# One loop over all laps, a wider class of packets from an earlier step, x loaded into the output's place and copied by ScalarE, b2 added by a product on TensorE

## The reference

```python
agg = segment_sum(edge_attr, dst, num_segments=6250)      # (200000, 128) -> (6250, 128)
h = concatenate([x, agg, u[batch]], axis=1)                # batch is all zeros: u[0] everywhere
h = relu(h @ W1 + b1)
y = x + (h @ W2 + b2)
return (y - mean(y)) / sqrt(var(y) + 1e-5)                 # over the 128 features
```

## Time and profile before

| | |
|---|---|
| median of 3 runs | 275.88 us (275.78 to 275.94) |
| the profiled execution: its own time | 276.12 us |
| its span, first to last instruction | 274.4 us |
| granted TensorE clock over the span | 0.938 |
| busy: TensorE, its weight loads | 213.2 us (78%), 168.7 us (61%) |
| busy: VectorE, ScalarE, GpSimd | 177.2 us (65%), 50.8 us (19%), 41.5 us (15%) |
| DMA | 110.06 MB, mean 401 GB/s |
| HBM read, written | 106.63 MB, 3.20 MB |

### The profile page before, as it was taken

One profiled execution on the slowest core, in us unless ns is written; L12 is line 12 of the kernel. 1 busy time (PEld: TensorE's weight loads), 2 busy tenths in 40 slices (PEclk: granted clock), 3 DMA queues, 4 the chain that ended last, 5 costly groups with the idle time before them and its releaser, 6 DMA issues.

```text
span 274.4 us, 15313 instructions
## 1 busy us (share of the span) xinstructions
PE 213.2 (78%) x6767; PEld 168.7 (61%) x6767; DVE 177.2 (65%) x435; ACT 50.8 (19%) x100; POOL 41.5 (15%) x49
## 2 busy tenths in 40 slices
PE   0874899987886449999884789895898897867872
PEld 0763687855655347877653658674766676655751
DVE  7842285793674997596874436959928769465542
ACT  0410122311211201122210211322022212121210
POOL 6400020030210012040300200300303003030020
PEclk9998699999999859999999599999599999999997
DMA  7999999999999999999999999999999999999994
GB/s 252 391 396 401 400 401 404 402 401 405 402 406 402 401 402 402 404 401 415 416 418 409 416 412 414 421 415 416 418 426 428 422 425 432 418 430 422 429 393 174
DMA packets 28863, 110.06 MB, mean 401 GB/s; under 512 B 2008, under 2 KB 3374, under 8 KB 26926
## 3 DMA queue, kind: packets, MB, share of 16 engines
q1 hardware_dynamic: 25588, 105.83, 95.9%
q10 hardware_dynamic: 3258, 4.00, 4.0%
HBM read 106.63 MB, written 3.20 MB: 400 GB/s over the span
## 4 chain that ended last, share of the span: by engine, by line
PE 58%; issue 13%; DVE 12%; DMA 12%; POOL 1%; ACT 1%; DVEq 1%; POOLq 0%; ACTq 0%
PE rows_ps L860 31%; PE cols_ps L872 14%; DMA slots<-in_edge_attr 12%; PE hid_ps L904 4%; PE hid_ps L886 3%; DVE tall_ids L687 3%; PE hid_ps L895 3%; PE hid_ps L880 2%; ACT rows L444 1%; DVE hot L615 1%; DVE z L678 1%; DVE first_of_pair L570 1%; POOL rstd L408 1%; DVE dst_local L583 1%; DVE high L696 1%
## 5 line engine op out<-in xcount | busy, mean ns | idle before, releaser
L860 PE MATMUL rows_ps<-slots,hot 64*32 64x128 f32 x6240 | 113.4, 285 | 35.7 <-issue 23.4
L860 PEld LDWEIGHTS rows_ps<-slots,hot 64*32 64x32 f32 x6240 | 93.6, 110 | 53.5 <-issue 50.7
L641 DVE TENSOR_TENSOR agg_t<-agg_t,cols_ps 128x128 f32 (+1 forms) x65 | 21.5, 331 | 84.1 <-PE cols_ps L872 83.8
L872 PE MATMUL cols_ps<-row_hot,rows 128*128 128x128 f32 (+1 forms) x260 | 56.3, 341 | 11.4 <-ACT rows L444 6.3
L615 DVE TENSOR_TENSOR hot<-edge_node,iota 128x768 f32<-128x768 f32 x65 | 61.8, 952 | 2.5 <-issue 1.6
L444 ACT ACTIVATE rows<-rows_ps 128x256 f32<-128x256 f32 x65 | 25.0, 384 | 177.3 <-PE rows_ps L860 170.1
L872 PEld LDWEIGHTS cols_ps<-row_hot,rows 128*128 128x128 f32 x260 | 40.8, 198 | 25.3 <-ACT rows L444 13.1
L408 POOL TENSOR_TENSOR rstd<-var_eps,minus_half 128x4 f32<-128x4 f32 (+1 forms) x13 | 16.6, 1275 | 196.7 <-DVE var_eps L672 196.7
L631 DVE TENSOR_TENSOR row_hot<-row_node,iota 128x256 f32<-128x256 f32 (+1 forms) x65 | 38.4, 591 | 0.0
L399 POOL TENSOR_TENSOR z<-x_rows,b_all 128x512 f32<-128x512 f32 (+1 forms) x13 | 17.2, 1323 | 29.8 <-PE hid_ps L880 29.8
L678 DVE TENSOR_SCALAR z<-z,moments,rstd (+1 forms) x49 | 17.2, 410 | 1.1 <-POOL rstd L408 1.0
(11 more groups left out here) (119 smaller groups left out, 70.3 us busy)
## 6 DMA issues: line engine op xcount, KB each, us to landing
slots<-in_edge_attr SPq DMA_DIRECT2D x65, 1536.0 KB, 14.9
x_rows<-in_x ACTq DMA_DIRECT2D x11, 256.0 KB
out<-z SPq DMA_DIRECT2D x11, 256.0 KB
dst_int<-in_dst SPq DMA_DIRECT2D x1, 384.0 KB, 3.9
dst_int<-in_dst ACTq DMA_DIRECT2D x1, 384.0 KB, 4.6
x_rows<-in_x ACTq DMA_DIRECT2D x1, 192.0 KB
out<-z SPq DMA_DIRECT2D x1, 192.0 KB
rest_slot<-in_edge_attr ACTq DMA_DIRECT2D x1, 128.0 KB, 8.5
```

Of the source, the lines that this page charges most:

```text
L641: V.tensor_tensor(cols, cols, cols_ps[:, 0:n], ALU.add).then_inc(added, 1)
L860: done = T.matmul(rows_ps[i][c * SPAN:(c + 1) * SPAN, h, 0:feats], hot[j][part, c * RUN + r, :], slots[part, j, c, r * feats:(r + 1) * fea ...
L872: done = T.matmul(cols_ps[:, 0:n], rows[i][:, h, :], row_hot[j][:, h, 0:n], start=(h == 0), stop=(h == HALVES - 1))
```

## The change

- `DENSE` goes from 30 to 25 and `TALL` from 50 to 48, so steps 25 to 29 come in pieces of 6144 instead of 3072 bytes, and steps 48 and 49 in pieces of 12288 instead of 6144.
- TensorE and VectorE each have one loop for all laps (`one_lap`). Every step but the last has 224 columns. `level2` stands behind the next `level1` throughout, but `level2` of a lap's fourth step stands ahead of the fifth `level1`, because the last three steps of a lap now share two sets of buffers (`SETS`).
- `rows_ps` has two sets instead of three. In the room, the turned x (`turn_bank`) and the second product (`y_bank`) get banks of their own.
- x is loaded into `z`, two laps ahead, and ScalarE copies it to `x_rows` (`stage_x`) for turning. GpSimd's `bias_add` is gone. `product2` begins with a product of a row of ones and b2 repeated four times, 512 columns wide, in the same sum.
- Blocks begin at row 128: block 0 now has the last 490 rows, in three pieces, and block 11 is a plain one.
- The extra product on iota in the last lap (L953 before) is gone, as are the waits of TensorE for `plan_made`.
- The ids of the `TALL` steps are turned one quarter at a time, in laps 3 to 6, and brought home in lap 7.
- VectorE and SyncE load `plan` and branch before the end: VectorE in the last lap behind the `add` of step 59, SyncE ahead of the last store.

```diff
-SETS = (0, 1, 0, 1, 2)
-DENSE_LAP = 6
-DENSE = DENSE_LAP * LAP
-TALL = 10 * LAP
+SETS = (0, 1, 0, 1, 1)
+DENSE = 5 * LAP
+TALL = 48
...
@@ sync
-            store(final)
-
             with sp.If(plan_now < 1):
+                store(final)
...
+            with sp.If(plan_now > 0):
+                store(final)
@@ gpsimd
+            G.memset(z[:, 0, :, :], 0.0).then_inc(x_zero, 1)
...
-            def bias_add(seq, i):
...
@@ scalar
             def load_x(seq):
+                if seq == 0:
+                    act.wait_ge(x_zero, 1)
                 i = seq % places
-                if seq:
-                    act.wait_ge(z_ready, seq)
...
+                for memory, home in pieces_of(i, x, lambda parts, r0, r1: z[parts, i, r0:r1, :].rearrange("p r f -> p (r f)")):
+                    act.dma_start(home, memory).then_inc(x_in[i % 2], 16)
+
+            def stage_x(seq):
+                i = seq % places
+                m = rows_of(i)
+                act.wait_ge(x_in[i % 2], x_landed(seq // places, i))
+                A.activation(x_rows[:, 0:m, :], z[:, i, 0:m, :], ACT.Copy).then_inc(x_staged, 1)
...
             for lap in range(laps):
                 for j in range(LAP):
                     t = lap * LAP + j
+                    if t:
                         copy_rows(t)
+                    if j == 1:
+                        if lap:
+                            relu(lap - 1)
+                        copy_x(lap)
+                    elif j == 3 and lap + 1 < final:
+                        load_x(lap + 2)
                     elif j == 4 and lap < final:
+                        stage_x(lap + 1)
@@ vector
+            with dve.Fori(1, laps - 1) as lap:
+                one_lap(lap, counts(lap), range(-1, LAP - 1))
+            last_at = step_bases((laps - 1) * LAP - 1, LAP)
+            one_lap(laps - 1, last_at, range(-1, 0))
+            def ending():
+                one_lap(laps - 1, last_at, range(0, LAP - 1))
+                add(held, 0, DENSE_COLS)
+                residual(final, final)
+                variance(final, final)
+                normalise(final, final)
...
+            plan_now = general_if(dve)
+            with dve.If(plan_now < 1):
+                ending()
                 general()
+            with dve.If(plan_now > 0):
+                ending()
@@ tensor
             def product2(seq, i):
...
+                T.matmul(y_bank[:, 0:n], ones[0:1, :], b2_rows[:, :, :].rearrange("a r f -> a (r f)")[:, 0:n], start=True, stop=False)
                 pe.wait_ge(hid_made, seq + 1)
                 for r in range(rows_of(i)):
-                    done = T.matmul(y_ps[:, r, :], hid[:, r * P:(r + 1) * P], w2_sb[:, :], start=True, stop=True)
+                    done = T.matmul(y_ps[:, r, :], hid[:, r * P:(r + 1) * P], w2_sb[:, :], start=False, stop=(r == rows_of(i) - 1))
...
+            def one_lap(lap):
                 counts(lap)
                 for j in range(LAP):
                     t = lap * LAP + j
                     if j == 4:
+                        level2(t - 1, j - 1, COLS)
                     level1(t, lap, j)
                     if j == 0:
+                        with pe.If(lap > 0):
+                            level2(t - 1, LAP - 1, COLS)
...
+                    elif j == 1:
+                        with pe.If(lap > 0):
+                            pe.wait_ge(added, lap * LAP + 1)
+                            product1_agg(lap - 1, start_of(lap - 1))
...
+                        level2(t - 1, j - 1, COLS)
+                        turn_x(lap, True)
+                    elif j == 2:
+                        with pe.If(lap > 0):
+                            product2(lap - 1, lap - 1)
+                        level2(t - 1, j - 1, COLS)
...
                     elif j == 3:
+                        level2(t - 1, j - 1, COLS)
...
+            with pe.Fori(0, laps) as lap:
+                one_lap(lap)
+            level2(held, LAP - 1, DENSE_COLS)
             pe.wait_ge(added, steps + 1)
             product1_agg(final, start_of(final))
             product2(final, final)
```

More of the change, by code:

```diff
@@ L726, in counts @@
                     dve.compute_val(lap + n)
-                return step_bases(lap * LAP, LAP)
-            def sparse_lap(lap):
-                at = counts(lap)
-                for j in range(LAP):
-                    t = lap * LAP + j
-                    mixed = not isinstance(lap, int) and j + AHEAD >= LAP
-                    add(t, at[j], False)
-                    if not isinstance(lap, int):
-                        if j == 2:
-                            residual(lap - 1, lap - 1)
-                            with dve.If(lap == TURN):
-                                turn_tall_ids()
-                        elif j == 3:
-                            variance(lap - 1, lap - 1)
-                        elif j == 4:
-                            normalise(lap - 1, lap - 1)
-                    make_hot(t + AHEAD, j + AHEAD, None if mixed else False)
@@ L747, in dense_lap, with one_lap @@
-            def dense_lap(lap):
-                at = counts(lap)
-                for j in range(LAP):
-                    t = lap * LAP + j
-                    add(t, at[j], True)
+                return step_bases(lap * LAP - 1, LAP)
+            turned_at = {-1: 0, 0: 1, 2: 2, 3: 3}
+            def one_lap(lap, at, steps_of):
+                looped = not isinstance(lap, int)
+                for j in steps_of:
+                    t = lap * LAP + j
+                    if j == 0 and looped:
+                        with dve.If(lap == JUDGE + 1):
+                            dve.wait_ge(bad_summed, 1)
+                            dve.wait_ge(level2_done, t + 1)
+                            V.tensor_copy(bad_total[:, :], bad_ps).then_inc(bad_read, 1)
+                            dve.wait_ge(bad_read, 1)
+                    add(t, at[j + 1], COLS)
```

318 lines of the change are left out of this document (121 added, 197 removed).

## The result

| | before | changed |
|---|---|---|
| median of the runs on one chip | 275.83 us (275.34 to 276.20, 6 runs) | 280.72 us (279.27 to 281.67, 6 runs) |
| ratio | | 1.0171, 95% interval 1.0151 to 1.0191 |
| the profiled execution, its span | 276.12, 274.4 us | 281.17, 279.4 us |
| granted TensorE clock | 0.938 | 0.963 |
| busy: TensorE, VectorE, ScalarE, GpSimd | 213.2, 177.2, 50.8, 41.5 us | 230.9, 180.9, 58.6, 21.2 us |

The account below looks back on a forecast made before the run. The edge stream was taken as the bound: load 64 lands 2.2 us earlier (packets 0.77, late engine 1.4), TensorE's last lap leaves 0.85, the tail takes 0.1, so 276.12 - 0.75 = 275.4, on the median 275.2 us; range 274.0 to 276.7.

Parts of the forecast that it names:

- a lap of TensorE is then ... 16.6 us: TensorE's lap in the loop, summed from operation prices with the b2 product: 16.6 us against 19 us of stream.
- the lateness inside of a lap ... is worked off in the next: TensorE's laps: lateness of up to 2 us at a lap's fifth step was to be gone in the next lap.
- what costs nothing: Part on wider level2, 0.86 us b2 product per lap, x copies, zeroing, id turning and branches: all claimed covered or free.
- The margin: TensorE's room in each lap against the stream's five steps, claimed as 2.4 us.
- TensorE's lateness as a rival: Last lap, level1 of step 64: late engine stays, TensorE bounds, level1 0.6 us later than before; 276.5 us, chance 0.18.
- The branch on VectorE: Last lap: VectorE stands 6 us fetching missing code, under 4 us costs nothing; 276.4 us, chance 0.15.
- The instruction packets: TensorE's queue: four or five packets of 16 KB before 60 us, none from 100 to 260 us.
- The stream: Edge loads: load 64 lands 2.2 us earlier, at 263.1 us, from larger packets and one loop together.
- The late engine: One DMA engine, some 1.4 us behind the others at the end, read as hit twice by code fetches; worth 1.4 us.
- The packets' rate: Steps 25 to 29 go from 403 to 415 GB/s, 48 and 49 from 415 to 426: load 64 0.77 us earlier.
- The tail: From level1 of step 64 to the end: 0.1 us longer, so the tail ends 0.75 us earlier.

Follow-up runs that it names:

- e6: Changed kernel with the judge's two reductions over the ids replaced by small copies, so the smallest and largest id aren't found: 276.52 us, ratio 1.0028.
- e7: Changed kernel without TensorE's product that adds b2, so b2 is missing from the output: 276.28 us, ratio 1.0016.
- e1: Changed kernel with VectorE's and SyncE's load of plan and branch put back behind the last normalise and last store: 279.97 us, ratio 1.0167.
- e15: Changed kernel with short judge (reductions replaced by copies), no b2, later second half of GpSimd's zeroing, and last block ahead of the branch: 275.87 us, ratio 1.0003.
- e2: Changed kernel with GpSimd's second group of memsets waiting for rows_made instead of local_made: 280.42 us, ratio 1.0170.
- e8: Kernel before with the change's two packet sizes (dense from step 25, tall from 48), its two loops changing over where they did: 275.17 us, ratio 0.9984.
- e4: Kernel before with the larger packets (DENSE 30 to 25, TALL 50 to 48), its second loop beginning a lap earlier: 276.52 us, ratio 1.0026.
- e13: Changed kernel with b2 added by GpSimd on z after ScalarE's copy, and no b2 product on TensorE: 277.22 us, ratio 1.0048.
- e14: e13 with GpSimd's second half of the zeroing after the rows are made and the last block ahead of the branch: 277.04 us, ratio 1.0045.
- e5: Changed kernel with JUDGE = 5 instead of 8, so the reading of the ids comes three laps earlier: 277.18 us, ratio 1.0063.
- e11: e10 with the judge in smaller pieces, one of four rows at the end of each step of laps 8 and 9: 282.50 us, ratio 1.0242.
- e9: Changed kernel with the whole judge spread over three laps: largest ids in lap 8, smallest in 9, the rest in 10: 279.76 us, ratio 1.0155.
- e10: e9 with GpSimd's second half of the zeroing after the rows are made and the last block ahead of the branch: 280.23 us, ratio 1.0162.
- e12: e6 with GpSimd's second half of the zeroing after the rows are made and the last block ahead of the branch: 276.76 us, ratio 1.0036.

## Why the prediction was wrong, step by step

- **The step that failed: "a lap of TensorE is then ... 16.6 us", with "the lateness inside of a lap ... is worked off in the next", under the heading of what costs nothing.** The lap measured 18.1 us, and the next 17.9. The sum's work is all there (five `level1` and `level2`, three wide products, `product2`, the turn of x): without its waits the lap is some 16.7 us. What the sum left out are the waits, in the lap of 219.02 0.19 us for one-hots, 0.68 for the `add` between the two `level2` in a row and 0.52 for ScalarE's copy, 1.4 us together. The margin was 1.0 us of a lap, not 2.4.
- **What the sum never had in it: the judge.** It went through the last lap as if TensorE entered it on time. The stand in lap 8 is in the timeline of before, 2.90 us with a half clock behind it; it cost nothing there because TensorE then regained 3.0 us in a lap and waited for rows again from step 54. Making the lap longer turned a stall that was free into 4 us. e6 and e7 show both halves of this.
- **The stall grew besides**, from 2.90 and 1.26 us to 4.94 us. I had not asked what the new order (`level2` of a step behind the next `level1`, one `cols_ps`) does to it.
- **TensorE's lateness as a rival** was in the text, but as 0.9 to 1.4 us inside the last lap. It took the right place, `level1` of 64 with the b2 product and two `level2` ahead, and a price less than half of the real one. The 3.65 us were carried in from lap 8.
- **The branch on VectorE** stood 4.55 us; the rival put its threshold at 4. Its sequencer took the branch (L836) at 259.0 and started the next instruction, at the head of the second copy (L839), only at 263.8; the load of `plan` ahead of it had taken 0.33 us:

```profile
L836 DVEq COMPARE_BRANCH  x1: 63/63/63, 259.0 to 259.0; - x1
...
L839 DVEq COMPARE_BRANCH  x1: 50/50/50, 263.8 to 263.8; - x1
```

  The trace agrees here with the Trainium skill (Runtime: NRT & Kernel Launch, Instruction fetch mechanics), that a taken branch whose target isn't in the window must fetch before it goes on: an instruction packet of 8 KB came in the stand, at 261.9. The packet alone proves little, as e1 has one at 260.0 and no stand. The stand cost nothing that e1 would show.
- **The instruction packets** came as forecast. TensorE's queue has five in the whole execution:

```profile
q8 instruction: 5, 0.08, 0.1%
```

  four before 48 us and one near the end, none from 48 to 260.
- **The stream**: forecast 2.2 us earlier. In the profiled execution load 64 was 1.0 us later, and in e15 1.2 us earlier. The loss lies ahead of step 25: its rows were in at 115.8 against 113.1 before, partly for the dip at the head (below), but still at 114.1 in e2, which hasn't the dip; what takes this 1.0 us stays open. From there to the landing of 64 the stream took 150.4 us instead of 152.2, and 149.3 in e15, so 1.8 to 2.9 us less, about what was forecast.
- **The late engine** was probably read rightly, and the trace of before has the place. Loads 41 and 42, issued at 166.3 and 169.4:

```profile
L332 SPq DMA_DIRECT2D slots<-in_edge_attr x1: 368/368/368, 166.3 to 166.3; - x1
...
DMA to landing us min/median/max: 9.5/9.5/9.5
...
L332 SPq DMA_DIRECT2D slots<-in_edge_attr x1: 367/367/367, 169.4 to 169.4; - x1
...
DMA to landing us min/median/max: 11.9/11.9/11.9
```

  They land at 175.8 and 181.3, 5.5 us apart, while the stream goes on at 415 GB/s in 175:181, and between them runs the packet that came alone, at 177.5. e8 has the same between steps 42 and 43, 5.9 us, with its lone packet at 180.2. None of the 14 kernels with one loop has more than 4.6 us between two landings from step 15 on. (e4, the third with two loops, can't be read here, since its stream had run dry.) This ties the two only by their time, in two kernels; no run moved the packet alone.
- **The packets' rate** was right: 418 GB/s in 115:132 us, where the kernel before had 408.
- **The tail** was forecast at +0.1 us and took +0.4. All of it lies behind the last `normalise`: from `level1` of 64 to there it took 6.33 us, 6.50 before, and from there to the span's end 3.15 instead of 2.53. What makes this end longer stays open; it is 2.8 us in e1 and e2, 3.2 in e7 and e15, and 2.3 to 2.4 in e13 and e14.

## What to carry to other kernels

A stall in the middle of a run is free only as long as the laps behind it can work it off: before you lengthen a lap of an engine that waits for a stream, list every stall upstream of the end, and divide it by the room that is left in a lap. Measure that lap from one start to the next in the timeline, where the engine is already late, and not as a sum of its operations; two sets of buffers or a single `cols_ps` add waits that no operation's price contains.

## What the runs showed of the hardware

- **GpSimd's memsets can hold up VectorE by 0.2 us or by 3.1.** In the head of the changed kernel two small operations of VectorE fell on GpSimd's zeroing:

```profile
8.79 3.44 POOL L407 MEMSET agg_t<- 128x512 f32 x8 [2.91 <-DVE dst_local L589]
8.89 3.38 DVE L593 TENSOR_SCALAR base_diag<-ident,base 128x64 f32<-128x64 f32 x1
9.06 3.22 DVE L595 TENSOR_TENSOR row_low<-low 128x4 f32<-128x4 f32 x1
```

  The same `base_diag` took 1.39 us in e1, 0.93 in e6, 0.47 in e5 and e7, and 0.25 in e2, where the memsets start after it. The steps between these are whole memsets: the eight memsets start 0.46 us apart, and `base_diag` ended 0.1 us behind the start of the second (e5), the third (e6) or the fourth (e1), or behind the end of the last (the changed kernel). The Trainium skill (GPSIMD Engine Reference, 1. Specifications) has GpSimd's way to the memory shared with VectorE, in contention with VectorE's instructions in a 2-port perf mode or with two inputs in it; the trace agrees, as the seven kernels with later memsets all have 0.25 or 0.26 us. In the profiled execution `level1` of step 0 started 3.3 us later than before (16.60 against 13.34), 2.9 of them for this, and loads 8 to 10 were issued 3.7 to 8.1 us later: 283 GB/s in 38:40 us, 132 in 44:46.
- **GpSimd's add does the same in the laps.** Beside it VectorE's `row_hot` took 1.71 us instead of 0.62 (e13), and 1.49 instead of 0.41 in the kernel before.
- **A wait ahead of a loop's turn** laid open what the turn costs VectorE's sequencer: 1.1 us of branches and register work and 1.2 us for one load of `bases`, 2.5 us in all, behind a piece of 0.55 us (e11).
- **A taken branch** over one copy of the last steps and the general version held VectorE for 4.8 us, from the branch to the first instruction at its target, with the stream at 420 GB/s (the changed kernel).
- **The clock falls in other places though the laps are the same.** Between 60 and 260 us e9 has one fall, at 119; e10, whose laps have the same instructions, has three, in 138:142, 193:197 and 213:217. Among the eleven runs of e15 the mean granted clock goes from 0.942 to 0.982. The spread of the times doesn't follow from this: e6, e7 and e12 vary by 0.4 to 0.7 us over their runs and the changed kernel by 2.4, but e8, whose TensorE is 0.1 us behind its rows at the end, varies by 3.1. What makes it stays open.
